# A transformer layer on one core: one stack load moved behind the next pair's maxima, and a weight-quantising unit moved later in the last batch

## The reference

```python
xn = _layernorm(x, axis=-1)                        # x: 8 x 1024 x 512, float32
x = x + attention(xn, W_attn, b_attn, W_proj, b_proj) + ffn(xn, w_gate, w_up, w_down)
# attention: 16 heads of 32, causal mask, softmax over the keys
#   att = softmax(where(causal, q @ k.T * 32 ** -0.5, -inf));  y = att @ v;  y @ W_proj + b_proj
# ffn: h = silu(Q(x) @ Q(w_gate).T) * (Q(x) @ Q(w_up).T);  Q(h) @ Q(w_down).T     (1408 wide)
# Q: each block of 16 values is divided by max|.| / 6, rounded to the grid
#    0, 0.5, 1, 1.5, 2, 3, 4, 6 with its sign, and multiplied back
```

## Time and profile before

| what | us |
|---|---|
| median of 3 runs | 3735.48 (3733.85 to 3745.34) |
| the profiled execution, by its own time | 3740.65 |
| its span, first to last instruction | 3738.8 |
| TensorE busy in it | 3660.0 (98%) |
| VectorE busy | 2638.5 (71%) |
| ScalarE busy | 1199.3 (32%) |

### The profile page before, as it was taken

The page is one execution under the profiler, slowest core; times in us unless marked ns, Lnnn a source line. Parts: engine busy times, 40 slices in busy tenths (PEclk is TensorE's granted clock), DMA queues, the critical chain, the costliest instruction groups (busy, mean ns, idle before and its releaser), DMA issues.

```text
span 3738.8 us, 63849 instructions
## 1 busy us (share of the span) xinstructions
PE 3660.0 (98%) x21836; PEld 2699.9 (72%) x21836; DVE 2638.5 (71%) x3834; ACT 1199.3 (32%) x2313; POOL 930.6 (25%) x462
## 2 busy tenths in 40 slices
PE   8999999999999999999999999999999999999999
PEld 6657657657656566566565578888888888888887
DVE  6675766766766766766766667777777777777776
ACT  2542532533523524514414412222222222222222
POOL 0560741642632724615615500000000000000000
PEclk9999999999999999999999999999999999999999
DMA  6525435335336245254256331100111110011110
GB/s 199 124 72 178 109 101 175 77 123 165 80 120 173 63 144 155 58 185 123 73 179 172 119 122 34 34 31 28 34 34 34 34 32 31 30 34 34 34 34 28
DMA packets 180526, 337.02 MB, mean 90 GB/s; under 512 B 42688, under 2 KB 50368, under 8 KB 179392
## 3 DMA queue, kind: packets, MB, share of 16 engines
q1 hardware_dynamic: 156096, 280.47, 26.5%
q10 hardware_dynamic: 24192, 53.49, 4.2%
HBM read 213.92 MB, written 118.43 MB: 89 GB/s over the span
## 4 chain that ended last, share of the span: by engine, by line
PE 90%; issue 2%; DMA 2%; DVE 2%; POOL 2%; ACT 1%; SPq 0%; ACTq 0%; DVEq 0%; POOLq 0%
PE f_ps L1523 26%; PE ps_dense L1016 13%; PE f_ps_o L1535 13%; PE ps_st L1072 9%; PE ps_s L1041 5%; PE ps_y L1093 4%; PE ps_dense L1180 4%; PE ps_dense L1093 3%; PE ps_dense L1111 3%; PE ps_dense L1041 2%; PE f_ps L1515 1%; PE ps_st L1079 1%; DMA stack<-mr 1%; POOL stage L585 1%; PE ps_s L1046 1%
## 5 line engine op out<-in xcount | busy, mean ns | idle before, releaser
L1523 PE MATMUL f_ps<-wgu,xqt 128*128 128x512 f32 (+1 forms) x4608 | 992.9, 373 | 1.4 <-DVE xqt L1383 1.4
L1523 PEld LDWEIGHTS f_ps<-wgu,xqt 128*128 128x128 f32 x4608 | 842.4, 188 | 123.0 <-DVE xqt L1383 1.7
L933 ACT ACTIVATE pt<-ps_st 128x512 f32<-128x512 f32 (+3 forms) x1152 | 550.4, 526 | 540.4 <-PE ps_st L1072 354.8
L653 DVE TENSOR_REDUCE mx<-ps_s 128x1 f32<-128x640 f32 (+3 forms) x512 | 523.8, 1023 | 212.2 <-PE ps_s L1046 203.1
L585 POOL TENSOR_TENSOR stage<-stage,pt 128x1536 f32<-128x1536 f32 (+2 forms) x176 | 519.1, 2950 | 15.2
L1535 PE MATMUL f_ps_o<-wd,hqt 128*128 128x512 f32 x2112 | 513.4, 396 | 0.2 <-DVE hqt L1409 0.2
L583 POOL TENSOR_TENSOR stage<-pt 128x1792 f32<-128x1792 f32 x64 | 256.5, 4009 | 882.6 <-ACT pt L933 882.6
L1535 PEld LDWEIGHTS f_ps_o<-wd,hqt 128*128 128x128 f32 x2112 | 392.6, 189 | 79.5 <-DVE hqt L1409 0.6
L1016 PE MATMUL ps_dense<-arena,wa 128*128 128x512 f32 x1536 | 384.1, 399 | 11.1 <-DVE rob L701 6.2
L1016 PEld LDWEIGHTS ps_dense<-arena,wa 128*128 128x128 f32 x1536 | 281.1, 189 | 73.7 <-issue 10.8
L653 DVE TENSOR_REDUCE mx<-ps_dense 128x1 f32<-128x128 f32 (+3 forms) x424 | 204.4, 482 | 87.5 <-PE ps_dense L1046 78.1
(11 more groups left out here) (135 smaller groups left out, 4943.1 us busy)
## 6 DMA issues: line engine op xcount, KB each, us to landing
qk_scratch<-stage SPq DMA_DIRECT2D x128, 512.0 KB, 2.8
stack<-qk_scratch SPq DMA_DIRECT2D x192, 256.0 KB
arena<-qk_scratch SPq DMA_DIRECT2D x192, 256.0 KB
xs<-in_L_attn_x SPq DMA_DIRECT2D x64, 256.0 KB, 3.6
rob<-in_L_attn_x ACTq DMA_DIRECT2D x64, 256.0 KB, 2.8
acc_scratch<-rob ACTq DMA_DIRECT2D x64, 256.0 KB, 2.2
xt<-in_L_attn_x SPq DMA_DIRECT2D x64, 256.0 KB, 2.6
at<-acc_scratch SPq DMA_DIRECT2D x64, 256.0 KB, 2.6
```

Source lines behind the costliest of these rows:

```text
L653: nc.vector.tensor_reduce(mx[:, h * ST + q:h * ST + q + 1], scores_bank(p, n)[:, 0:(q + 1) * P], axis=AX.X, op=ALU.max, negate=True).then_ ...
L933: nc.scalar.activation(exps(kt)[:, h, q - kt * P:q - kt * P + n], ps_st[:, w % ST_RING, 0:n], ACT.Exp, scale=SCALE).then_inc(st_exp, 1)
L1523: last = nc.tensor.matmul(ps[:, SLOT[c], gu, 0:n].rearrange("p (j n) -> p j n", n=P), xqt[:, a, k], wgu[:, b, gu * FC + f // P:gu * FC + ( ...
```

## The change

Two places. In every batch SP loads after V7 only slot 2; the seven loads of slot 3 stand in the loop over the pairs, at `p == 0`, behind the `mr` writes of the second pair and ahead of the wait for the first pair's exponentials. In the last batch the steps of the third unit stand later: scaling behind QK11 instead of QK7, magnitudes ahead of QK12 instead of QK8, rounding behind QK13 instead of QK8, transposes behind QK14 instead of QK9, high and low halves at QK15 instead of QK10, and the stores behind QK15 instead of QK11. The load of the unit stays behind QK6.

```diff
-                if i == 11 and final:
+                if i == 15 and final:
                     store_unit(2)
...
-            later = stack_loads(2) + stack_loads(3)
+            later = stack_loads(2)
...
                 if p + 1 < PAIRS:
                     maxima(p + 1)
+                if p == 0:
+                    for args in stack_loads(3):
+                        load(*args)
                 if p:
                     spread(p - 1)
...
-                    if use == ("QK", 7):
+                    if use == ("QK", 11):
                         scale_unit(2)
-                    if use == ("QK", 8):
+                    if use == ("QK", 13):
                         round_unit(2)
-                    if use == ("QK", 10):
+                    if use == ("QK", 15):
                         low_of_unit(2)
...
-                if (kind, i) == ("QK", 8) and final:
+                if (kind, i) == ("QK", 12) and final:
                     magnitudes(2)
-                if (kind, i) == ("QK", 10) and final:
+                if (kind, i) == ("QK", 15) and final:
                     high_of_unit(2)
...
-                if use == ("QK", 9) and final:
+                if use == ("QK", 14) and final:
                     transpose_unit(2)
```

## The result

| | median us | runs | lowest to highest |
|---|---|---|---|
| before, same chip | 3736.42 | 4 | 3733.85 to 3745.34 |
| changed | 3763.01 | 4 | 3755.34 to 3764.83 |

The changed kernel takes 1.0063 times as long (95% interval 1.0041 to 1.0085). It is slower, by 26.6 us between the medians and by about 24 by the ratio; 3725 was forecast, with a range up to 3738. Its profiled execution is the slowest of its four runs, 3764.83 us by its own time, with a span of 3763.0, which is 24.2 more than the span before. TensorE's mean granted clock fell from 0.996 to 0.990.

A forecast was written before the change was run, and what follows sets the result against it. TensorE, busy 98% of the span, was taken as the bound. 13.7 + 4.6 - 9.1 - 2.0 + 4.4 = 11.6 us gained; for the median 3735.5 - 11.6 + 1.5 = 3725 us, range 3711 to 3738.

The forecast's parts named there:

- The `mr` waits: Start of each batch's second pair: TensorE's eight waits for the maxima writes go, returning all of 13.7 us.
- the three clock drops: Behind three of the second pairs' starts: low-clock stretches costing 1.55 us each would go, 4.6 us gained.
- Where the `den` rows land: Second pair, first batch: denominator rows land at 134.3 behind the loads, making VectorE's reciprocal 2.1 us late (1.3 to 2.8).
- the slower rival: Second pairs: denominator rows over 3 us late, clock falls, 3.75 us in each of seven batches; 3744 us, chance 0.12.
- The price of a microsecond of lateness: Reciprocal in the second pair: 0.8 us of lateness are free, the rest is paid in full.
- The clock: Late reciprocal in seven second pairs: 1.3 us each, 9.1 us together (3.5 to 14), with no low clock included.
- The last batch: Second pair of the last batch, where feed-forward weights share the DMA engines: late reciprocal costs 2.0 us.
- The third unit: Last batch: 7.3 us gained from QK7 to QK10, less 2.1 and 0.8; net gain 4.4 us (2.5 to 6).
- The half drop: Last batch, TensorE's 1.5 us stall at the unit's new place: half of a clock drop's 1.55 us, 0.8, set aside.
- Sum: Whole kernel: 11.6 us gained off the profiled execution, giving 3729, or 3725 us for the median.

The follow-up runs named there:

- e7_one_six: The changed kernel with one of slot 3's seven loads ahead of the second pair's maxima and six behind; 3728.89 us, ratio 0.9977 to before.
- e5_fill: The changed kernel with eight more matmuls on TensorE just ahead of the second pair's `MAX` step; 3743.73 us, ratio 1.0006 to before.
- e2_unit_only: The kernel before with only the third unit's steps moved in the last batch, stack loads unmoved; 3734.05 us, ratio 0.9977.
- e11_best: The changed kernel with the first pair's reciprocal behind the maxima's split, unit scaling behind QK12, magnitudes ahead of QK14; 3718.24 us, ratio 0.9945 to before.
- e1_stack_only: The kernel before with only slot 3's loads moved behind the maxima, the unit where it was; 3769.3 us, ratio 1.0067.
- e3_den_first: The changed kernel with the fifth load set (slot 0) also moved, behind the issue of the `den` rows; 3724.8 us, ratio 0.9954 to before.

## Why the prediction was wrong

- **The `mr` waits.** Right. All 13.7 us came back, in every batch, and the three clock drops at those starts went as well (4.6 us).
- **Where the `den` rows land.** Right in its mechanism, too small in its size. They were put at 134.3 and landed at 135.7, since the engines were full for 0.9 us longer (share 0.86 still in 132 to 133) and the last row came some 2.5 us behind the traffic. The reciprocal waited 3.2 us in the first batch and 2.7 or more in the others, not 2.1. The condition of the slower rival, landing past 135.2, was met. It had 0.12.
- **The price of a microsecond of lateness.** Right where the clock stays up: "0.8 us of lateness are free, and the rest is paid" gives 2.2 us for 3.0, and the pair without a drop is 21.77 - 19.59 = 2.2 longer. At 2.07 us of waiting `e7_one_six` confirms it too. The larger lateness makes this term 15.2 us in seven batches instead of 9.1.
- **The clock. This is the step that failed:** "Cost: 2.1 - 0.8 = 1.3 us in each of seven batches, 9.1 us (bounds 0.5 and 2.0: 3.5 and 14)." Neither the sum nor the bounds held a low clock behind the new stall. The prediction let itself be led by one stall, the 2.01 us of the earlier trace rows, behind which the clock stayed up; that was VectorE's wait, while TensorE stood only 0.98 us there (the row stands below this list). In the changed kernel it stood 1.6 to 2.2 us in the seven ordinary batches. And where the slower rival did price the clock, it used 1.55 us a drop, from the shorter low stretches of before. Here a drop lasts 6.8 or 10.2 us. The pairs with 6.8 last 24.75 on average, 3.0 over the 21.77 without one; those with 10.2 last 26.1, 4.3 over it. The low clock costs 0.42 to 0.44 us for each of its microseconds, and 0.45 to 0.46 at the old drops (1.54 and 1.57 for 3.4). The seven pairs are 37.2 us over their old length; 37.2 - 15.2 = 22 us of it is the clock, and `e5_fill` gives 22.2 back with the reciprocal as late as before.
- **The last batch.** 2.0 us were taken; the second pair lasts 10.1 over 19.59, since the reciprocal waits 6.35 us, TensorE stands 5.31 and the clock is low for 13.6. Why the rows land up to 10.8 us after their issue in this batch was not tested.
- **The third unit.** Right: 7.3 us gained in QK7 to QK10, a price of 2.5 (2.1 forecast), no drop behind TensorE's 1.30 us stall (0.8 set aside). 4.8 gained, 4.4 forecast; `e2_unit_only` confirms the sign (7.5 by the medians, with an interval of 5 to 12). The half drop was set aside because the clock fell behind 1.53 and not behind 1.50 us. That was no boundary: the drops behind 1.17 and 1.19 us in `e2_unit_only` show it.
- **Sum.** 6 us from the larger lateness, 22 from the clock and 8 from the last batch are 36 us, less 0.4 for the unit: the distance from the forecast 11.6 us of gain to the 24 us of loss. The slower rival named the right place and mechanism, and gave 3744. It was too cheap, because it put each ordinary batch at 3.75 us and it was 5.3.

TensorE in the fourth pair of the last batch, before the change, behind VectorE's wait of 2.01 us:

```profile
2052.45 0.33 PE L1051 MATMUL ps_dense<-ident,mx 128*128 128x128 f32 x1 [0.98 <-DVE mx L653]
```

On the clock's price the Trainium skill (TensorE: Matmul & The Clock Gate, "HAM oscillation — how this bites in real kernels") charges half of the time spent at the low level. This case's pairs gave 0.42 to 0.46, a little less.

The table that the Trainium skill has in the same page (TensorE: Matmul & The Clock Gate, "Why this matters for your kernels") warns only of idle gaps longer than those of the seven ordinary batches. By that advice TensorE's stalls of 1.6 to 2.2 us would have kept its clock. The trace speaks against it: in six of the seven they didn't, and the measurement decides.

## What to carry to other kernels

When transfers move to another place in a queue, find the next small transfer behind them and what stands queued behind the instruction that waits for it: the price is what TensorE then idles, and if that comes near the length behind which a profile of the kernel has ever shown the clock fall, add a low stretch of several microseconds to the bounds at once. Here that length went down to 1.17 us when more profiles were read. Take the instruction that waits off the path (a reciprocal whose result is wanted only later goes behind the one whose result is wanted now) rather than the transfer. The transfer then has more room, but an end of it remains: in the last batch of `e11_best` the next work queued behind the reciprocal was held. Ask how long TensorE stands, not how long the engine before it does.

## What the runs showed of the hardware

- The same stall may or may not bring the clock down, and no single length divides the cases. TensorE stood 1.96 us in the sixth batch of the changed kernel and 2.16 us in the fourth of `e1_stack_only` and kept 2.4 GHz; after 1.64 us in the seventh batch of the changed kernel, and after 1.17 and 1.19 us in `e2_unit_only`, it had 1.2 GHz. The stalls of 0.56 to 1.04 us in `e7_one_six` (seven batches) and that of 1.30 us at the unit had no drop.
- The clock can fall when TensorE is already busy again: 1.9 us after the stall in the seventh batch, about 1.8 us after the gap in the fourth batch of `e2_unit_only`.
- The low stretch can be much longer than the idle time behind which it begins: 6.8 to 13.6 us for 1.6 to 5.3 us in the changed kernel, with TensorE busy in nearly all of it from its restart on (9.74 of 10.3 us in the first batch). What ends it was not settled by these runs.
- A small transfer behind queued loads is late out of proportion to its size. `den` rows took 2.3 us to the last landing with no loads ahead (`e3_den_first`), and 3.7, 6.5 and 7.8 us behind the fifth load set and two, five and six of the moved loads of 256 KB: about 1 us for each of these.
